# Reordering the tail of a fused Mamba and mixture-of-experts block on one core: the first batch's experts set among the second batch's router steps

## The reference

```python
h = _layernorm(x) * (1 + ca) + sa
x = x + ga * attn(h)                     # two selective scans, projections, a norm
h = _layernorm(x) * (1 + cb) + sb
Sm = swapaxes(softmax(einsum('bsh,eh->bse', h, Wg)), 1, 2)
G, I = top_k(Sm, 64)                     # per batch and expert
ex = take_along_axis(h[:, None], I[..., None], axis=2)
out = G[..., None] * (gelu(ex @ W1 + b1) @ W2 + b2)
x = x + gb * zeros.at[batch, I].add(out)
```

## Time and profile before

| | |
|---|---|
| Runs | 610.56, 611.45, 612.16 us; median 611.45 |
| Profiled execution | 610.64 us, of which the span from first to last instruction 608.9 |
| Busy in the span | PE 503.9, PEld 415.4, DVE 467.1, ACT 442.7, POOL 331.7 us |
| Mean granted clock of TensorE | 0.933 |

### The profile page before, as it was taken

One profiled execution on the slowest core, in us unless ns is written; L12 is line 12 of the kernel. 1 busy time (PEld: TensorE's weight loads), 2 busy tenths in 40 slices (PEclk: granted clock), 3 DMA queues, 4 the chain that ended last, 5 costly groups with the idle time before them and its releaser, 6 DMA issues.

```text
span 608.9 us, 9243 instructions
## 1 busy us (share of the span) xinstructions
PE 503.9 (83%) x3378; PEld 415.4 (68%) x3378; DVE 467.1 (77%) x709; ACT 442.7 (73%) x845; POOL 331.7 (54%) x155
## 2 busy tenths in 40 slices
PE   3569979969899996989988969698776666989997
PEld 3246757759687685878855858697665554788696
DVE  5857799769887785898899859989999997484032
ACT  2469868999997799999867899889797710443060
POOL 3105648769875686796657759667586651100000
PEclk9898999998999999799999889799899899685999
DMA  7030222212322212132221202212452240000101
GB/s 251 0 108 36 70 69 71 89 52 76 101 80 95 71 70 69 67 110 71 72 69 43 94 38 93 86 70 70 137 174 71 70 138 1 0 2 2 34 1 36
DMA packets 17885, 43.46 MB, mean 71 GB/s; under 512 B 1328, under 2 KB 7600, under 8 KB 17584
## 3 DMA queue, kind: packets, MB, share of 16 engines
q1 hardware_dynamic: 17840, 42.87, 21.4%
HBM read 41.56 MB, written 1.31 MB: 70 GB/s over the span
## 4 chain that ended last, share of the span: by engine, by line
PE 39%; ACT 27%; DVE 25%; issue 6%; POOL 2%; DMA 1%; DVEq 0%; ACTq 0%; POOLq 0%
ACT dBuT L572 12%; DVE area L975 10%; PE yT L1190 9%; PE pro L1190 9%; PE yT L1194 8%; ACT dA L565 7%; PE dBu L1194 6%; PE dBu L1190 5%; DVE area L971 3%; POOL hc L481 2%; PE pro L1194 2%; DVE area L763 1%; ACT th L533 1%; ACT pre L540 1%; ACT area L555 1%
## 5 line engine op out<-in xcount | busy, mean ns | idle before, releaser
L481 POOL TENSOR_TENSOR hc<-area 128x1024 f32<-128x1024 f32 x127 | 304.0, 2396 | 157.8 <-DVE area L971 90.9
L572 ACT ACTIVATE dBuT<-area,bT 128x256 f32<-128x256 f32 x508 | 215.1, 498 | 13.8 <-PE dBu L1194 13.8
L1194 PE MATMUL dBu<-ident,dBuT 128*128 128x128 f32 x1024 | 149.3, 284 | 42.5 <-DVE area L975 23.2
L565 ACT ACTIVATE dA<-area,Aneg 128x1024 f32<-128x1024 f32 x128 | 146.2, 1143 | 20.4 <-DVE area L975 13.5
L1194 PEld LDWEIGHTS dBu<-ident,dBuT 128*128 128x128 f32 x1024 | 119.7, 145 | 56.8 <-issue 22.2
L1194 PE MATMUL yT<-ident,hc 128*128 128x128 f32 x1024 | 140.6, 283 | 1.7 <-POOL hc L481 1.4
L1194 PEld LDWEIGHTS yT<-ident,hc 128*128 128x128 f32 x1024 | 120.9, 145 | 20.0 <-issue 16.0
L975 DVE TENSOR_TENSOR_SCAN area<-dA,area,dBu 128x512 f32<-128x512 f32 x64 | 81.8, 1278 | 4.6
L971 DVE TENSOR_TENSOR_SCAN area<-dA,area,dBu 128x512 f32<-128x512 f32 x64 | 81.8, 1278 | 4.2
L971 DVE TENSOR_TENSOR_SCAN area<-dA,dBu 128x512 f32<-128x512 f32 x64 | 77.2, 1206 | 7.9 <-PE dBu L1194 7.5
L975 DVE TENSOR_TENSOR_SCAN area<-dA,dBu 128x512 f32<-128x512 f32 x64 | 77.1, 1205 | 6.6 <-PE dBu L1194 6.0
(11 more groups left out here) (226 smaller groups left out, 577.0 us busy)
## 6 DMA issues: line engine op xcount, KB each, us to landing
area<-c_rows SPq DMA_DIRECT2D x64, 512.0 KB, 3.6
dBuT<-w_in SPq DMA_DIRECT2D x1, 2048.0 KB, 9.0
wp<-wpack_in SPq DMA_DIRECT2D x1, 1030.0 KB, 7.3
x<-x_in SPq DMA_DIRECT2D x2, 512.0 KB, 6.5
hc<-bcast_in SPq DMA_DIRECT2D x1, 1024.0 KB, 10.2
out<-x SPq DMA_DIRECT2D x4, 256.0 KB, 2.3
hT<-w_in SPq DMA_DIRECT2D x1, 512.0 KB, 7.3
acc<-w_in SPq DMA_DIRECT2D x1, 512.0 KB, 7.1
```

Of the source, the lines that this page charges most:

```text
L481: g_.tensor_tensor(hc[:, e % 3, :], hs[:, e % 3, :], Cb[:, g % 3, :], ALU.mult).then_inc(hc_done, 1)
L565: nc.scalar.activation(dA[:, e % 3, :], delta[par][:, half, :], ACT.Exp, scale=Aneg[:, dr, half, s:s + 1]).then_inc(da_ready, 1)
L572: return nc.scalar.activation(dBuT[:, g % 2, n, :], duT[par][:, n, :], ACT.Copy, scale=bT[:, par, n, s:s + 1])
L1194: return nc.tensor.matmul(out, in_, ident[:, :] if idn is None else idn, start=start, stop=True, is_transpose=True, skip_group_check=True)
```

## The change

On VectorE all eight one-hot blocks of batch 0 are built ahead of the last output items, and `slots_shift(0)` moves ahead of norm stage 7. On PE and ScalarE the experts of batch 0 are no longer worked off by the loop that batch 1 uses, but by lists written out: the first steps of the experts (one-hot transposes 0 to 3, slot logits, up of pairs 0 and 1) stand ahead of LT of batch 1, the others between the items of its router, with one scatter between QE and CT. ScalarE preloads the function table of Exp after LT. The waits for W1 and W2 are apart.

```diff
@@ ScalarE: order of batch 0 (keep_eo is moved up, unchanged)
-            gathered_tokens(0)
-            for k, j in NORM_ITEMS[0:2]:
-                item_a(k, j, 1)
-            slots_softmax(0)
-            logits_exp(1)
-            for q in range(NPAIR):
-                hidden(0, q)
-                keep_turned(0, 2 * q)
-                keep_turned(0, 2 * q + 1)
-                if q:
-                    keep_down(0, q - 1)
-                if q >= 2:
-                    keep_eo(0, q - 2)
-            keep_down(0, NPAIR - 1)
-            keep_eo(0, NPAIR - 2)
-            keep_eo(0, NPAIR - 1)
+            gathered_tokens(0)
+            keep_turned(0, 0)
+            keep_turned(0, 1)
+            slots_softmax(0)
+            hidden(0, 0)
+            keep_turned(0, 2)
+            keep_turned(0, 3)
+            for k, j in NORM_ITEMS[0:2]:
+                item_a(k, j, 1)
+            nc.scalar.preload_act_table(ACT.Exp)
+            keep_turned(0, 4)
+            keep_turned(0, 5)
+            logits_exp(1)
+            hidden(0, 1)
+            keep_down(0, 0)
+            hidden(0, 2)
+            keep_turned(0, 6)
+            keep_turned(0, 7)
+            keep_down(0, 1)
+            keep_eo(0, 0)
+            hidden(0, 3)
+            keep_eo(0, 1)
+            keep_down(0, 2)
+            keep_down(0, 3)
+            keep_eo(0, 2)
+            keep_eo(0, 3)
@@ VectorE
-            build_onehot(0, range(0, 6))
+            build_onehot(0, range(NBLK))
...
             norm_stage(1, 6)
-            build_onehot(0, range(6, NBLK))
+            slots_shift(0)
             norm_stage(1, 7)
-            slots_shift(0)
             slots_weights(0)
@@ TensorE: experts(b) keeps only its form for b = 1; the tail
             gather(0, range(NBLK))
-            norm_items(NORM_ITEMS[0:2])
-            slot_logits(0)
-            norm_items(NORM_ITEMS[2:3])
-            experts(0)
-            down(0, NPAIR - 1)
-            turn_eo(0, NPAIR - 2)
-            turn_eo(0, NPAIR - 1)
-            for q in range(NPAIR):
+            turn_onehot(0, 0)
+            turn_onehot(0, 1)
+            slot_logits(0)
+            pe.wait_ge(s_w1, 16)
+            up(0, 0)
+            turn_onehot(0, 2)
+            turn_onehot(0, 3)
+            up(0, 1)
+            norm_items(NORM_ITEMS[0:2])
+            turn_onehot(0, 4)
+            turn_onehot(0, 5)
+            norm_items(NORM_ITEMS[2:3])
+            pe.wait_ge(s_w2, 48)
+            down(0, 0)
+            norm_items(NORM_ITEMS[3:4])
+            up(0, 2)
+            down(0, 1)
+            turn_onehot(0, 6)
+            turn_onehot(0, 7)
+            turn_eo(0, 0)
+            up(0, 3)
+            norm_items(NORM_ITEMS[4:5])
+            turn_eo(0, 1)
+            norm_items(NORM_ITEMS[5:6])
+            down(0, 2)
+            scatter(0, 0)
+            down(0, 3)
+            turn_eo(0, 2)
+            turn_eo(0, 3)
+            norm_items(NORM_ITEMS[6:])
+            for q in range(1, NPAIR):
                 scatter(0, q)
             gather(1, range(NBLK))
```

More of the change, by code:

```diff
@@ L1459, in experts @@
             def experts(b):
[L1461 to L1465, removed]
-                for q in range(NPAIR):
[L1467 to L1475, removed]
+                pe.wait_ge(x2_ready, 2)
+                for q in range(NPAIR):
+                    up(b, q)
+                    turn_onehot(b, 2 * q)
                     turn_onehot(b, 2 * q + 1)
@@ L1478, in experts @@
                         down(b, q - 1)
-                    if b == 0 and q in (1, 2):
-                        norm_items((NORM_ITEMS[4:5], NORM_ITEMS[6:7])[q - 1])
                     if q >= 2:
```

## The result

| | before | after |
|---|---|---|
| Runs | 610.56 to 612.16 us, median 611.22 (4) | 596.02 to 598.31 us, median 597.89 (4) |
| Ratio after to before | | 0.9775, 95% interval 0.9750 to 0.9799 |
| Profiled execution | 610.64 us, span 608.9 | 597.98 us, span 596.2 |

The change takes 13.3 us off; 15.0 were forecast, 596.4 us, with 590.5 to 602.5 as the range.

The account below looks back on a forecast made before the run. PE was taken to bound the piece between gathers: 62.8 us = 37.6 work + 9.4 idle + 15.8 clock. Reordering -20.0 and half clock +4.9 give -15.0, rounded; 611.45 - 15.0 = 596.4 us, range 590.5 to 602.5.

Parts of the forecast that it names:

- (a): VectorE, ahead of the last output items: building two one-hot blocks early costs nothing; 0.6 us of cover is left.
- (b): PE, gather of batch 0: its last two blocks follow at once, so it ends at 514.1 instead of 522.1.
- (c): PE behind the gather: transposes 0 and 1 hide ScalarE's 0.78 us copy; up(0,1) ends at 520.5, W1 isn't waited for.
- (e): PE before batch 1's router: waits 1.6 us for normed rows; LG waits for ScalarE's copy, then runs 524.2 to 526.1.
- (d): VectorE: slots_shift fits ahead of norm stage 7, normed rows come at 521.97 as before; margin 1.5 us behind stage 6.
- (f): ScalarE: three function table loads instead of one before the second batch, 1.28 us each, costing no more than 0.2 us.
- (g): Batch 1's router chain with batch 0's experts between, at full clock: gather(1) starts at 550.1 instead of 570.0, -20.0 us.
- the clock: PE around batch 1's router: half clock from 527 to 537 and some 3.5 us after QT and QE, +4.9 us.
- The part carried over: From the start of gather(1) to the end: left alone by the change, 38.9 us as before.
- rival B: Drop at 519 to 527 holds 17 us, a second follows around batch 1's slot logits: -8, 603.4 us; chance 0.18.
- rival A: No clock drop at all in the rearranged piece on PE: -20.0, 591.4 us; chance 0.2.
- these two: PE's router logits, 1.92 us, and slot logits, 0.96 us: durations from before, not doubled for half clock.

Follow-up runs that it names:

- Experiment 1: The kernel before with only the one-hot blocks of batch 0 all built early, all else in its old order: 617.9 us, ratio 1.0112.
- experiment 3: The changed kernel with slots_shift(0) put back behind norm stage 7: 605.0 us, ratio 0.9903 to before.
- experiment 5: The changed kernel without the preload of Exp's function table: 597.4 us, ratio 0.9781 to before.
- experiment 6: The changed kernel with 9 products of 256 columns added on PE whose results nobody reads: 593.5, 605.2, 606.1 and 607.9 us, and 607.8 when run once more.

## Why the prediction was right

*(a), (b).* Right. The gather ran through in 6.9 us, and the hole was gone. Experiment 1 shows that this is no gain by itself.

*(c), (e).* Right within 0.6 us: PE waited 0.96 us for the normed rows where 1.6 was put, and 0.32 for ScalarE's copy ahead of LG.

*(d).* Right, and of more weight than said: stage 7 began 12.2 us behind the piece's start, as in before (12.6), and the price of the other place is 7 us, not the margin of 1.5 (experiment 3).

*(f).* The sum, nothing, was right, one reason was not. The forecast took the preload to be what keeps the table's load out of the router's chain; without it the load is early just as well (experiment 5).

*(g) and the clock.* The walk put QT 31.9 us and gather(1) 47.8 us behind the piece's start (539.1 and 555.0 less 507.2). They came at 31.8 and 47.6. The first spell was put at 527 to 537 and lay, less the 1.0 us of later start, at 527.4 to 537.2. The second was put behind QT and QE, 3.5 us, and lay on the scatters behind CT, 3.2 us. The row of eight transposes brought the clock back as it had in before. That this is so close has luck in it: experiment 6 shows the same instructions 10 us apart by the clock alone, and in its profile of 607.8 us the clock stayed down through a row of eight transposes.

*The part carried over.* This is the term that was off. It was put at 38.9 us and took 40.4, since the clock fell at 565.8, behind the slot logits of batch 1 and in the first up-products, for 3.3 us; the end of the prediction names it as what would make the sum wrong, and rival B had half of it. The repeat of the changed kernel has it too, from 565.0 to 568.4. With the 1.0 us by which the piece began later, and the 0.2 by which the piece came out shorter than put, it makes the difference between -15.0 and the profile's -12.7. Why the clock falls at this place in the changed kernel and not in before, no run settles.

*The rule weighed.* The Trainium skill ("TensorE: Matmul & The Clock Gate", "What's actually happening") has the clock follow how busy PE was. By it, read as busy time, rival A (591.4 us) was the outcome; 597.9 was measured, and the clock fell at 528 with PE busy without a wait since 524.95. Read so, it can't tell the changed kernel from the one with wide logits: the same waits and the same length of LG (1.92 and 1.97 us), and the clock falls behind the one and stays through the other.

*One duration.* "I don't double these two", with the clock "partly at a half" as the reason, misreads the rows. In before the clock was at 1.00 from 523.7 on, so 0.96 and 1.92 us are times at full clock, and at half clock they do double: in experiment 1, at a granted 0.50, LG took 3.56 us and the slot logits 1.71, with LG's 16 weight loads in 3.53 us instead of 1.86. It had no effect on the sum, since both ran at full clock in the changed kernel.

## What to carry to other kernels

On a bound TensorE, count idle time and half clock apart before costing a reorder: here they gave 6.9 and 8.2 us. Look for stretches in which it is busy with narrow products behind full weight loads; widening the products to the time that the load takes anyway costs next to nothing (1.97 us instead of 1.92), and took away the drop behind them. By itself it gained nothing here: the old order became 1.7 us slower, the new one stayed as it was until down(0,2) was moved as well. And a hole must be filled, not moved: taking away the wait, the drop or the late block that a later wait had covered only brings PE to the next one sooner, in two of these experiments with a longer spell of half clock behind it.

## What the runs showed of the hardware

- Logits products of 8 columns with a full weight load: 16 records in 1.92 us at a granted 1.00 (changed kernel), 3.56 us at 0.50 (experiment 1). With 64 columns, 1.97 us at 1.00.
- Behind the router's logits the granted clock fell to 0.50 in five profiles of five where they had 8 columns, and in none of three where they had 64, with the same neighbours.
- Behind the slot logits of batch 1 it fell in five profiles of nine with 8 columns, and in one of three with 64 (3.3 us at 0.50 from 561.4).
- The same program's piece took 44.1 us at a mean granted clock of 1.00 and 54.6 us at 0.78 (experiment 6).
- The load of a function table, 1.28 us, ran ahead of ScalarE's wait for the data of the operation that needs it (525.81, the operation at 527.44, experiment 5).
